# Edge attention on a graph: one of every 24 row gathers of GpSimd becomes a one-hot product on TensorE

## What is computed

```
q = (x @ Wq + bq).reshape(n, H, C)
k = (x @ Wk + bk).reshape(n, H, C)
v = (x @ Wv + bv).reshape(n, H, C)
e = (eattr @ We).reshape(-1, H, C)
kj = k[src] + e
alpha = jnp.sum(q[dst] * kj, axis=-1) / jnp.sqrt(jnp.float32(C))
m = jax.ops.segment_max(alpha, dst, num_segments=n)
a = jnp.exp(alpha - m[dst])
s = jax.ops.segment_sum(a, dst, num_segments=n)
a = a / (s[dst] + 1e-16)
vj = v[src] + e
out = jax.ops.segment_sum(a[..., None] * vj, dst, num_segments=n)
```

## Time and profile before

| | us |
|---|---|
| median of three runs | 6829.01 |
| the profiled execution's own time | 6818.34 |
| its span, first to last instruction | 6816.5 |
| TensorE busy | 4422.8 (65%) |
| VectorE busy | 4366.3 (64%) |
| GpSimd busy | 4726.5 (69%) |
| ScalarE busy | 1118.9 (16%) |

### The profile page before, as it was taken

The page is one execution under the profiler, slowest core; times in us unless marked ns, Lnnn a source line. Parts: engine busy times, 40 slices in busy tenths (PEclk is TensorE's granted clock), DMA queues, the critical chain, the costliest instruction groups (busy, mean ns, idle before and its releaser), DMA issues. The chain is left out here.

```text
span 6816.5 us, 149747 instructions
## 1 busy us (share of the span) xinstructions
PE 4422.8 (65%) x36620; PEld 3475.0 (51%) x36620; DVE 4366.3 (64%) x15732; ACT 1118.9 (16%) x4722; POOL 4726.5 (69%) x5116
## 2 busy tenths in 40 slices
PE   7996666666666667666666666667666666666665
PEld 5775444444444446444444444446444444444444
DVE  5556666666666666666666666666666666666666
ACT  3222111111111112111111111112111111111111
POOL 1224777777777775777777777775777777777776
PEclk9995555555555555555555555555555555555555
DMA  4553333333333333333333333333333333333333
GB/s 128 159 159 96 95 95 95 96 95 95 95 96 95 96 95 98 95 95 95 95 95 95 95 95 95 95 96 97 95 95 95 95 95 96 95 95 95 96 96 80
DMA packets 687682, 675.79 MB, mean 99 GB/s; under 512 B 369234, under 2 KB 506388, under 8 KB 687636
## 3 DMA queue, kind: packets, MB, share of 16 engines
q0 software_dynamic: 161600, 320.52, 18.3%
q1 hardware_dynamic: 496944, 301.76, 16.3%
q10 hardware_dynamic: 29092, 52.97, 2.6%
HBM read 652.96 MB, written 21.67 MB: 99 GB/s over the span
## 5 line engine op out<-in xcount | busy, mean ns | idle before, releaser
L1621 POOL DMA_INDIRECT Gall<-KV,sdn x4848 | 4590.0, 947 | 1517.0 <-issue 1380.9
L754 DVE TENSOR_TENSOR kj<-Gall,pE 128x512 f32<-128x512 f32 x603 | 414.4, 687 | 1973.4 <-DMA Gall<-KV,sdn 1971.3
L963 PE MATMUL pG<-O,vals 128*66 128x42 f32 (+1 forms) x10736 | 1291.9, 308 | 0.7 <-ACTq L1242 0.7
L963 PEld LDWEIGHTS pG<-O,vals 128*66 128x66 f32 (+1 forms) x10736 | 1200.8, 223 | 47.4 <-ACT vals L1002 28.4
L948 PE MATMUL pY<-fw,Ob 128*42 128x6 bf16 (+1 forms) x4800 | 255.1, 176 | 1139.9 <-DVE cr L807 1139.9
L994 ACT ACTIVATE vals<-dd 128x16 f32<-128x16 f32 (+1 forms) x606 | 131.6, 217 | 4679.5 <-DVE dd L834 4671.0
L948 PEld LDWEIGHTS pY<-fw,Ob 128*42 128x42 bf16 x4800 | 220.4, 121 | 1192.9 <-issue 1192.9
L896 PE MATMUL pE<-bd,ea 128*128 128x256 f32 x1212 | 739.9, 714 | 13.6 <-PEq L1242 13.6
L955 PEld LDWEIGHTS pM<-Mb,OTs 42*128 42x128 bf16 x4800 | 176.3, 101 | 921.1 <-issue 921.1
L901 PE MATMUL pE<-bd,ea 128*128 128x256 f32 x1212 | 642.8, 634 | 0.0
L955 PE MATMUL pM<-Mb,OTs 42*128 42x6 bf16 (+1 forms) x4800 | 209.9, 163 | 514.2 <-DVE df L825 511.8
(11 more groups left out here) (223 smaller groups left out, 6539.9 us busy)
## 6 DMA issues: line engine op xcount, KB each, us to landing
db<-D SPq DMA_DIRECT2D x606, 256.0 KB
ea<-in_ea SPq DMA_DIRECT2D x606, 128.0 KB
Gall<-KV,sdn POOLq DMA_INDIRECT x4848
db<-D ACTq DMA_DIRECT2D x202, 256.0 KB, 3.5
qw<-QT SPq DMA_DIRECT2D x1818, 5.2 KB
dr<-in_dr SPq DMA_DIRECT2D x1212, 4.0 KB
ea<-in_ea SPq DMA_DIRECT2D x202, 64.0 KB, 3.3
sdn<-in_sdn SPq DMA_DIRECT2D x606, 12.0 KB
```

Of the source, the lines that this page charges most:

```text
L754: return e.tensor_tensor(kj[:, :, :], G[u][:, :, 0:64], pE[u][:, :].rearrange("p (j c) -> p j c", c=64), ALU.add)
L963: return e.matmul(out[0:AR, 0:W], vals[u][:, j, 0:AR], O[u][:, j, :], start=j == 0, stop=j == T - 1)
L1621: e.indirect_dma_start(G[u][:, j, :], None, kvtab, bass.IndirectOffsetOnAxis(ap=sdn[u][:, j:j + 1], axis=0)).then_inc(s_g[u], 16)
```

## The change

In every third attention step GpSimd gathers only seven tiles (`LAST` is the eighth). The eighth tile's rows are selected on TensorE from a copy of the table in SBUF, `KVS`, which takes the place of the staging tile: 50 tiles of 128 rows by 128 floats. The tiles are taken in 13 quads of four (the last has two). A source index is split into a key (quad and row within a tile) and a quarter (which tile of the quad). VectorE compares the keys of the 128 edges, broadcast to all partitions (`kb`), with partition and quad number (`oh`), and gets a 128 by 128 one-hot for each quad. TensorE multiplies each by the quad's 128 by 512 floats, and accumulates the 13 products in one bank (`gp`). This work is spread over the three steps before it is needed, in pieces of 4, 4 and 5 quads. VectorE then picks the right quarter of the 512 columns with four masked operations (`sel`, six instructions), straight into the place where the gather would have put the rows. The first block treated in this way is 3, the last 201, so 67 in each pass.

The keys are made once: the mean pass collects the eighth tile's sources (`src`), and after the mean layer's node phase TensorE transposes them, VectorE computes the keys, and SyncE stores them in HBM (`K16`) and later loads one block's keys for every picked block (`load_keys`, 128 values broadcast to 128 partitions), after the other loads of a step.

Because `gp` occupies the bank `pG`, the sums of `agg` and the scale factor move to the bank `pS`, which also holds `aT` and `Fb`. That adds two waits: the scale factor's product waits for `fm`, and `facc` waits for the `aT` of the same step. Scratch tiles of the setup now lie in `KVS`. In the diff, hunks that only rename or place things are left out.

```diff
+LAST = T - 1
...
+    QUADS = z.quads
+    order_q = list(range(QUADS - 2)) + [QUADS - 1, QUADS - 2]
+    PIECE = [QUADS // 3, QUADS // 3, QUADS - 2 * (QUADS // 3)]
+    FROM = [0, PIECE[0], PIECE[0] + PIECE[1]]
+    KG = -(-SM // 4)
...
+    KVS = sb("KVS", [128, NT, 128])
...
+    srcT = sb("srcT", [128, 4 * KG])
+    kb = sb("kb", [128, 128], I16)
+    oh = [sb(f"oh{u}", [128, PIECE[2], 128]) for u in range(3)]
...
+    pQd = pM[:, 6 * T + W:6 * T + W + QUADS]
+    pPick = pG[:, :].rearrange("p (i c) -> p i c", i=4)
+    pSumS = pS[:, 256:256 + W]
...
+        for k, q in enumerate(order_q):
+            if k == q and k:
+                continue
+            m = QUADS - 2 if k == 0 else 1
+            e.tensor_scalar(pQd[:, k:k + m], iof[:, q:q + m], 128.0, None, ALU.mult).then_inc(su_V, 1)
+        e.tensor_copy(prow[:, :], pmi[:, :]).then_inc(su_V, 1)
+        e.memset(srcT[:, :], 0.0).then_inc(su_V, 1)
+        e.tensor_copy(ioW[:, :], iof[:, 0:W]).then_inc(su_V, 1)
+        e.tensor_copy(ioq[:, :], ioi[:, 0:4]).then_inc(su_V, 1)
...
+    def sync_keys(e):
+        e.wait_ge(key_V, 4)
+        e.dma_start(K16.rearrange("(g r) m -> r g m", g=4),
+                    key_n.rearrange("p (g m) -> p g m", g=4)).then_inc(s_kn, 16)
+
+    def tensor_keys(e, ready):
+        for sm, v in ready:
+            e.wait_ge(sm, v)
+        for g in range(4):
+            p = e.transpose(pQ[0:KG, 128 * g:128 * g + 128], srcT[:, KG * g:KG * g + KG], ident[:, :])
+        p.then_inc(key_P, 1)
+
+    def vector_keys(e):
+        e.wait_ge(key_P, 1)
+        e.tensor_copy(key_i, pQ[0:KG, :]).then_inc(key_V, 1)
+        e.wait_ge(key_V, 1)
+        e.tensor_scalar(key_hi, key_i, 9, 7, ALU.logical_shift_right, ALU.logical_shift_left).then_inc(key_V, 1)
+        e.tensor_scalar(key_lo, key_i, 127, None, ALU.bitwise_and).then_inc(key_V, 1)
+        e.wait_ge(key_V, 3)
+        e.tensor_tensor(key_n, key_hi, key_lo, ALU.add).then_inc(key_V, 1)
...
-            e.activation(stg[:, g, 0:m, 0:128], kv_bank[c % 2][:, 0:128 * m].rearrange("p (t c) -> p t c", t=m),
+            e.activation(KVS[:, cells(c), :], kv_bank[c % 2][:, 0:128 * m].rearrange("p (t c) -> p t c", t=m),
...
-                "V": ["A kj", "A vj", "B fhi", "B fm", "B flo", "B cr", "Z OT", "A prod", "A alpha", "C d1", "C d",
-                      "Z cont", "Z last", "A flag", "A O", "B X", "B Mhi", "B Mm", "B Mlo", "B df", "C vals",
+                "V": ["A sel", "A kj", "A vj", "B fhi", "B fm", "B flo", "B cr", "Z OT", "A prod", "A alpha", "C d1", "C d",
+                      "Z cont", "Z last", "A flag", "A O", "Z oh", "B X", "B Mhi", "B Mm", "B Mlo", "B df", "C vals",
                       "D facc", "D acc", "A scan"],
-                "P": ["B Fb", "A q", "D agg7", "B Mn", "Z e", "A aT", "B Me"],
+                "P": ["B Fb", "A q", "A gp", "D agg7", "B Mn", "Z e", "A aT", "B Me"],
...
-                "V": ["C acc", "Z O", "Z OT"],
+                "V": ["C acc", "Z src", "Z O", "Z OT"],
...
+        first_pick = 2 + z.peel
+        pick_slot = first_pick % 3
+        s_k = sem(f"{name}_k") if att else None
+        sel_V = sem(f"{name}_sel") if att else None
+        sums = [pSumS, pSumS, pSumS] if att else [pG, pQ, pY]
...
+        def picks(s):
+
+            return s.slot == pick_slot and not (isinstance(s.i, int) and s.c < first_pick)
+
+        def rows_landed(e, s):
+            if s.slot == pick_slot:
+                full = first_pick // 3
+                n = s.times(16 * (T - 1), 16 * (T - 1 + full))
+                if isinstance(s.i, int) and s.c < first_pick:
+                    n = s.times(16 * T, 16 * T)
+                e.wait_ge(s_g[s.slot], n)
+            else:
+                ge16(e, s_g, T, s)
...
+        def v_src(e, s):
+            ge16(e, s_i, 1, s)
+            return e.tensor_copy(srcT[:, bass.ds(s.value(), 1)], sdn[s.slot][:, LAST:T])
...
+        def sel_at(s, k):
+            return s.times(5, k + 1 - 5 * (first_pick // 3))
+
+        def v_sel(e, s, inc, n):
+            u = s.slot
+            to = G[u][:, LAST, :]
+            e.tensor_scalar(quarter[:, :], sdn[u][:, LAST:T], 7, 3, ALU.logical_shift_right,
+                            ALU.bitwise_and).then_inc(sel_V, 1)
+            e.wait_ge(sel_V, sel_at(s, 0))
+            e.tensor_tensor(msk[:, :], ioq[:, :], quarter[:, :].to_broadcast([128, 4]),
+                            ALU.is_equal).then_inc(sel_V, 1)
+            e.wait_ge(sel_V, sel_at(s, 1))
+            after(e, "P", "gp", s - 1)
+            e.tensor_scalar(to, pPick[:, 0, :], msk[:, 0:1], None, ALU.mult).then_inc(sel_V, 1)
+            for k in range(1, 4):
+                e.wait_ge(sel_V, sel_at(s, k + 1))
+                i = e.scalar_tensor_tensor(to, pPick[:, k, :], msk[:, k:k + 1], to, ALU.mult, ALU.add)
+                if k < 3:
+                    i.then_inc(sel_V, 1)
+            i.then_inc(inc, n)
+
+        def v_oh(e, s):
+            k = (s.slot - pick_slot) % 3
+            m, f = PIECE[k], FROM[k]
+            if k == 0:
+                e.wait_ge(s_k, s.times(16, 16 * (2 - first_pick // 3)))
+            return e.scalar_tensor_tensor(
+                oh[s.slot][:, 0:m, :], kb[:, :].unsqueeze(1).to_broadcast([128, m, 128]), prow[:, 0:1],
+                pQd[:, f:f + m].unsqueeze(2).to_broadcast([128, m, 128]), ALU.subtract, ALU.is_equal)
...
-            ge16(e, s_g, T, s)
+            rows_landed(e, s)
+            if picks(s):
+                after(e, "V", "sel", s)
...
+                after(e, "P", "aT", s + 3)
...
+        def p_gp(e, s):
+            k = (s.slot - pick_slot) % 3
+            after(e, "V", "oh", s)
+            hold(e)
+            if k == 0 and picks(s):
+                after(e, "V", "sel", s)
+                hold(e)
+            for n in range(PIECE[k]):
+                q = order_q[FROM[k] + n]
+                m = min(4, NT - 4 * q)
+                p = e.matmul(pG[:, 0:128 * m], oh[s.slot][:, n, :],
+                             KVS[:, 4 * q:4 * q + m, :].rearrange("p t c -> p (t c)"),
+                             start=k == 0 and n == 0, stop=k == 2 and n == PIECE[k] - 1)
+            return p
...
+            v_sel(e, s0, dV, 1)
...
+            if made(at):
+                p_gp(e, at).then_inc(pP, 1)
+            else:
+                missing(e, "P", t, "gp", "gp")
             if "D" in on:
+                after(e, "V", "fm", bt)
+                hold(e)
                 after(e, "V", "acc", dt - 1)
                 hold(e)
-                p_fac(e, dt)
+                p_fac(e, dt, pFacS)
...
+        def load_keys(e, s):
+            if not (isinstance(s.i, int) and s.c == first_pick):
+                after(e, "V", "oh", s - 4)
+                hold(e)
+            e.dma_start(kb[:, :], K16[bass.ds(s.value(), 1), :].to_broadcast([128, 128])).then_inc(s_k, 16)
...
+            if att and picks(s + 2):
+                load_keys(e, s + 2)
...
-            for j in range(T):
+            for j in range(T - 1 if picks(s) else T):
```

More of the change, by code:

```diff
@@ L195, in build @@
                  "base", "base1", "over", "base2", "tbase", "tblock", "n0", "n1", "n2", "ntr", "me0", "onb",
-                 "cb", "cbh0", "cbh1", "rowf", "rowf4", "row1", "row2", "row12", "rowin", "thirds", "below", "third", "rowbase", "narrow", "iop"] + [f"qz{u}" for u in range(3)]
+                 "cb", "cbh0", "cbh1", "rowf", "rowf4", "row1", "row2", "row12", "rowin", "thirds", "below", "third", "rowbase", "narrow", "iop", "quads", "quads1", "quads2", "prow", "srcT", "ioW", "ioq"] + [f"qz{u}" for u in range(3)]
                 + [f"flg{u}" for u in range(3)] + [f"one{u}" for u in range(3)])
@@ L551, in query_A @@
             e.wait_ge(own["P"], pP["qs", c])
-            e.activation(stg[:, g, 0:m, 128:192], both[:, :, 0:64], ACT.Copy).then_inc(own["A"], 1)
+            e.activation(stg[:, g, 0:m, :], both[:, :, 0:64], ACT.Copy).then_inc(own["A"], 1)
             e.activation(SQ[:, cells(c), :], both[:, :, 64:128], ACT.Copy).then_inc(own["A"], 1)
@@ L556, in query_A @@
             e.wait_ge(own["A"], pA["qf", c])
-            e.activation(stq[:, g, 0:m, 0:64], stg[:, g, 0:m, 128:192], ACT.Copy).then_inc(own["A"], 1)
+            e.activation(stq[:, g, 0:m, 0:64], stg[:, g, 0:m, :], ACT.Copy).then_inc(own["A"], 1)
         def sync(e):
@@ L1242, in missing, with made @@
             e.sem_inc(prog[k], m - n)
+        def made(s):
+            return not isinstance(s.i, int) or s.c >= first_pick - 3
         def vector_step(e, t, on):
@@ L1255, in vector_step @@
                 else:
-                    missing(e, "V", t, "O", "OT")
+                    missing(e, "V", t, "src", "OT")
                 return
             if "A" in on:
-                v_kj(e, at).then_inc(pV, 1)
+                if picks(at):
+                    v_sel(e, at, pV, 1)
+                v_kj(e, at).then_inc(pV, 1 if picks(at) else 2)
                 v_vj(e, at).then_inc(pV, 1)
             else:
```

(18 more changed lines are left out.)

86 lines of the change are left out of this document (50 added, 36 removed).

## The result

The changed kernel takes **7677.89 us** (median of 4 runs, 7675.67 to 7678.83) beside 6828.85 us for the kernel before: 1.1241 times as long, 95% interval [1.1227, 1.1255]. The forecast was 6630 us in a range of 6575 to 7160. Sign and size are wrong, and the range missed.

What follows compares the result with a forecast made beforehand. GpSimd's gathers, one every 1.25 us, were taken as the bound. From 6818.3 us: 251 saved by dropped gathers, 42 added for the clock, 10 for small terms, giving 6619; the median lies 10.7 higher: 6630, range 6575 to 7160.

Steps and rivals of the forecast that it cites:

- the ring at full clock: Loop from one `scan` through TensorE and VectorE to the next: 8.6 us a step with TensorE at full clock.
- GpSimd's 9.58: GpSimd's 23 gathers in three attention steps, 1.25 us each: at least 9.58 us a step.
- from `Mn` 2.6: Full-clock loop's last part: `Mn`, then VectorE's chain from `X` to `scan`, taken to end last, 2.6 us.
- the gap shrinks: TensorE's pause between pieces: shorter when TensorE is late, so the clock stays up more often; 9.65 us a step forecast.
- The first rival: In `gp`: clock falls in every gap, each piece works 3.9 us at half; 10.55 us a step, 7170 us; 24%.
- the bound that I gave myself: TensorE's half-clock work must stay under 1.95 us a step for the loop to stay under GpSimd's gathers.
- fourth rival: GpSimd's gathers alone set the time, clock full whenever needed: 6588 us; counted as the lower half of the 50% main case.
- The floor: GpSimd's gathers as the only bound, with small terms of 10 us: 6829 - 251 + 10 = 6588 us.
- the stretch from the scale factor to the end of L936: Part of TensorE's work in the half-clock loop, taken as 2.4 us of 14.9 us a step.
- 9.97 us a step: Upper end of the in-between rival: TensorE and VectorE's loop at 9.75 to 9.97, 6690 to 6815 us; 16%.

Runs made afterwards that it cites:

- the kernel with fillers: Changed kernel plus two matrix products that nothing reads, behind `Me` on TensorE: 6669.91 us, 0.9779 of the kernel before.
- oh_first: Changed kernel with `oh` made ahead of `O` on VectorE: 6864.09 us beside 6819.59; on slower chips 1.0532 to 1.0548 of the kernel before.
- gp_after_aT: Changed kernel with the product's piece moved behind `aT` on TensorE, no fillers: 6663.34 us, 0.9765 of the kernel before; on slower chips 1.0459 and 1.0450.

## Why the prediction was wrong

**What held.** 4647 gathers. Prices: `oh` 0.74 (512 elements) and 0.88 (640), for 0.75; the product at full clock 4.0 us a step, for 3.9. `sel` took 2.1 us, for 1.75. The first piece of a group waits for it 1.15 us more (231.2 us in 201 groups), for 1.2. `load_keys` in time. And, as far as it can be seen, the ring at full clock: with `O`'s wait it is 8.6 + 1.0 = 9.6, and the kernel with fillers takes 9.8 us a step (102 in 1000 us). This confirms little, for GpSimd's 9.58 lies at the same place.

**The first step that failed: "from `Mn` 2.6, since there VectorE's own chain from `X` to `scan` ... ends last."** I took `X` as the head of that chain. It is `O`, which stands ahead of `X` on VectorE and waits for `agg` of three blocks back. In the old trace it never waited, so it was in none of the rows I summed; but the change puts 5 us of product ahead of `agg` in TensorE's order. The wait was in the code (line 800) and became one of the ring's links. With `O` 0.56 and `oh` 0.74 to 0.88 behind `agg`, the end of `agg` (1515.21 + 1.15) to `Fb` (1520.01) takes 3.65 us instead of the 2.6 from `Mn`: about 1.0 us a step. I had filed `oh` under VectorE's load, where it fits, and not under the ring, where it counts. Moving `oh` away showed 0.67 us of it. Moving the piece took all of the wait, but the piece itself left that part of the ring too. What `O`'s own 0.56 us costs was not tried alone.

**The second: "the gap shrinks ..., the clock is kept more often, and the ring gets faster ... Such a system settles near GpSimd's pace."** The gap did shrink, to 1.2 us ahead of `Fb` and 0.5 ahead of `Me`, and the clock fell in nearly every step all the same. The first rival's mechanism is what came, with 2 x 1.67 = 3.3 us of half-clock work a step for its 3.9. Its own time, 10.55 us, plus the 1.0 us of the missed wait is 11.55 against 11.36 measured. Of the two this one decided that the kernel became slower: with fillers the missed wait is still there, and the time is 6670. Half clock without the missed wait would be 8.6 + 1.67 = 10.27 us a step, some 7000 us, an estimate from the prediction's own sum and the 1.67 measured; that is slower too, but inside the full range of 6575 to 7160. What carried the time beyond the range is the missed wait on top. The two errors may also feed each other: with `oh` moved away the clock rose to 0.866, and with the piece behind `aT` to 0.85, with no filler. Of the bound that I gave myself, 1.95 us of half-clock work, the missed wait alone ate 1.0 x 2, that is all of it.

The Trainium skill, "TensorE: Matmul & The Clock Gate", Part 1, has it that an idle stretch of TensorE brings the throttle back. Read as in the prediction, that gave its fourth rival, 6588, which did not come. In these traces the clock fell behind pauses of 0.5 and 1.2 us, and in a moment of work. The measurement decides; what the rule says of the release (activity lifts it) agrees, as the piece of 1509.70 shows.

**The floor.** The kernel with the piece behind `aT` is bound by GpSimd and takes 6663, not 6588. GpSimd's idle time before a gather is 1515.1 / 4647 = 0.326 us; in the kernel before it is 1517.0 / 4848 = 0.313. The difference times 4647 is 61 us, most of the 75. Why it grew was not tried.

**The range** missed since rivals were single. Two mechanisms of one ring add; the case "rival 1 with another link late" had no chance of its own. Two slips in the sums change nothing: at half clock the stretch from the scale factor to the end of L936 is 2.5 us (1505.07 to 1507.57), not 2.4, and 9.97 us a step is 6821 us by the prediction's own sum, not 6815.

## What to carry to other kernels

When work is put into an engine's order, list every operation of every engine that waits for anything behind that place, also those that never waited before: an operation with no idle time in the old trace had slack, not freedom. Sum the new ring through all of them, in their engine's order, and not from the operation that was last before. Where TensorE is in the ring, its clock is a term that can feed on the ring's own idle time; then price both levels together with each other late link, look first for a place in the order behind everything that others wait for, and fill idle time with dummy products only if there is none.

## What the runs showed of the hardware that was not expected

TensorE's clock fell to 1.2 GHz in steps in which it was 83% busy, with no idle stretch over 1.2 us in most of them; two dummy products in that gap (1.13 us a step) raised the mean granted clock from 0.803 to 0.956 and saved 1012 us.

A ring of this kind can hold two patterns in one execution (clock 0.83 with 376 GpSimd instructions in 500 us, and 0.91 with 400), and its time spreads over 3% between six runs, where the other kernels repeat within 0.5%.

On four of the chips every kernel of this family that ran there was slower: the kernel before by some 3.8 us a step (9100 to 9160 us, for 6820 to 6829 on the others), `oh_first` and `gp_after_aT` by 4.5 to 4.8. Differences between the variants, which are large on the others, shrink there (`oh_first` and `gp_after_aT` lie 3% apart on the first kind and 1% on this one). The cause is open. A time is worth reading only beside the kernel before on the same chip.
